# Gated slot attention after the FFN: logits and read-out share one PSUM tensor, and three engines get new orders

## The reference

```python
q = _swish((x @ Wq).reshape(b, t, H, K)); k = _swish((x @ Wk).reshape(b, t, H, K))   # H = 4, K = 64
v = (x @ Wv).reshape(b, t, H, V)
f = jax.nn.log_sigmoid((x @ Wf).reshape(b, t, H, M)) / 8.0
s = 1.0 - jnp.exp(f)
def step(carry, inp):                       # over t, one sequence has 512 steps
    hk = hk * ge[:, :, None, :] + k_t[..., :, None] * s_t[..., None, :]
    logits = jnp.einsum('bhk,bhkm->bhm', q_t * scale, hk)
    p = jax.nn.softmax(logits, axis=-1)
    hv = hv * ge[..., :, None] + s_t[..., :, None] * v_t[..., None, :]
    o_t = jnp.einsum('bhm,bhmv->bhv', p, hv)
o = o * jax.lax.rsqrt(jnp.mean(o * o, axis=-1, keepdims=True) + 1e-5) * g_norm_w
return o.reshape(b, t, H * V) @ Wo
```

## Time and profile before

| | |
|---|---|
| Median of 3 runs | 3388.84 us (3388.57 to 3389.33) |
| The profiled execution: its own time | 3388.84 us |
| its span | 3387.1 us |
| Attention phase, first to last o_raw | 1465.2 to 2408.7 us, 128 operations |
| Busy over the whole span | TensorE 94%, VectorE 78%, ScalarE 49%, GpSimd 38% |
| Granted TensorE clock in 100 us stretches of 1500 to 2400 us | 1.00 |

### The profile page before, as it was taken

One profiled execution on the slowest core, in us unless ns is written; L12 is line 12 of the kernel. 1 busy time (PEld: TensorE's weight loads), 2 busy tenths in 40 slices (PEclk: granted clock), 3 DMA queues, 4 the chain that ended last, 5 costly groups with the idle time before them and its releaser, 6 DMA issues. The chain is left out here.

```text
span 3387.1 us, 102619 instructions
## 1 busy us (share of the span) xinstructions
PE 3176.5 (94%) x36736; PEld 2723.2 (80%) x36736; DVE 2655.2 (78%) x4369; ACT 1669.7 (49%) x4554; POOL 1302.7 (38%) x2170
## 2 busy tenths in 40 slices
PE   5999999999989999889999999999799999999999
PEld 4888888888866666578888888888588888888888
DVE  7999999999962323268888888888699999999998
ACT  3333333333325656578888888888333333333332
POOL 3333333333324343345555555555333333333332
PEclk9999999999989999989999999999799999999999
DMA  3111111111115555533333333333111111111111
GB/s 85 54 54 51 56 51 53 53 53 54 51 52 200 195 200 195 194 93 109 102 107 107 102 106 108 102 107 103 55 53 56 51 53 54 51 56 51 56 51 46
DMA packets 224965, 290.57 MB, mean 86 GB/s; under 512 B 25460, under 2 KB 191732, under 8 KB 224888
## 3 DMA queue, kind: packets, MB, share of 16 engines
q1 hardware_dynamic: 224888, 289.52, 27.0%
HBM read 171.97 MB, written 117.44 MB: 85 GB/s over the span
## 5 line engine op out<-in xcount | busy, mean ns | idle before, releaser
L578 PE MATMUL mid_ps<-xT_hl,w_hl 128*128 128x128 f16 x12288 | 728.7, 219 | 0.0
L425 PE MATMUL res_ps<-w_hl,midT_hl 128*128 128x256 f16 x6144 | 712.5, 273 | 1.2 <-DVE x_out L546 1.2
L578 PEld LDWEIGHTS mid_ps<-xT_hl,w_hl 128*128 128x128 f16 x12288 | 697.9, 98 | 0.5
L382 POOL TENSOR_TENSOR var_eps<-moments,eps_col 128x1 f32<-128x1 f32 x384 | 110.1, 287 | 1481.7 <-DVE moments L378 1481.7
L425 PEld LDWEIGHTS res_ps<-w_hl,midT_hl 128*128 128x128 f16 x6144 | 589.6, 98 | 65.5 <-DVE midT_hl L533 1.7
L486 ACT ACTIVATE midT_hl<-mid_ps 128x1024 f16<-128x1024 f32 x256 | 262.2, 1024 | 695.9 <-PE mid_ps L589 695.9
L512 DVE TENSOR_TENSOR_SCAN runmax<-restart,logits_ps 128x1024 f32<-128x1024 f32 x256 | 581.4, 2271 | 3.5 <-PE logits_ps L567 3.4
L397 ACT ACTIVATE xn_hl<-xc,rstd 128x256 f16<-128x256 f32 x384 | 194.2, 506 | 432.9 <-POOL rstd L387 351.6
L372 DVE BATCH_NORM_STATS2 stats<-x_in 128x6 f32<-128x256 f32 x384 | 161.8, 421 | 294.7 <-DMA x_in<-x 290.0
L533 DVE SCALAR_TENSOR_TENSOR midT_hl<-mid_ps,midT_hl 128x1024 f16<-128x1024 f32 x256 | 313.6, 1225 | 15.6 <-ACT midT_hl L486 7.8
L517 DVE TENSOR_TENSOR step<-runmax 128x1024 bf16<-128x1024 f32 x256 | 315.4, 1232 | 7.9
(11 more groups left out here) (143 smaller groups left out, 6188.9 us busy)
## 6 DMA issues: line engine op xcount, KB each, us to landing
projected<-qkfv_out SPq DMA_DIRECT2D x128, 512.0 KB, 2.9
qkv<-projected SPq DMA_DIRECT2D x128, 384.0 KB, 3.4
x<-x_out SPq DMA_DIRECT2D x256, 128.0 KB, 1.8
x_in<-x SPq DMA_DIRECT2D x256, 128.0 KB, 2.2
x_res<-x SPq DMA_DIRECT2D x256, 128.0 KB, 2.1
x_in<-in_L_attn_x SPq DMA_DIRECT2D x128, 128.0 KB, 2.0
x_res<-in_L_attn_x SPq DMA_DIRECT2D x128, 128.0 KB, 2.1
gate<-projected SPq DMA_DIRECT2D x128, 128.0 KB, 3.1
```

The source lines that it names most:

```text
L425: last = nc.tensor.matmul(dst, left(lp, k), right(rp, k), start=(k == 0 and lp == rp), stop=(k == blocks - 1 and lp == 1))
L578: nc.tensor.matmul(mid_ps[t.slot][:, cols], w1_hl[:, wp, k, cols], xT_hl[:, t.ring, xp, k], start=(c % PER_BANK == 0 and k == 0 and wp == xp),
```

## The change

Logits and read-out share the first 256 columns of one PSUM tensor, bank_rows; `logits` of tile s then waits for o_raw of tile s-2 (which has read them) and `read_out` of tile s-1 for logit of tile s. The transposes of o and the decay column share another, bank_16: `transpose_o` waits for the decay column to be read, the column sums of tile s+2 for oT of tile s-3. Their waits before are gone. The lists of ScalarE, VectorE and TensorE are in another order: ScalarE squares before it copies bank_T; VectorE adds and decays Hk before it masks; TensorE makes the logits before the transposes of k and S, and the state update before A and B. No operation is added or dropped, and GpSimd's and SyncE's lists stay.

```diff
--- before.py
+++ after.py
@@ -725,15 +725,14 @@
             def fb(name, shape, dt=f32):
                 return scope.enter_context(nc.sbuf_tensor(name, shape, dt))
 
-            bank_logits = psum(scope, "bank_logits", BANK)
+            bank_rows = psum(scope, "bank_rows", BANK)
             bank_pair = psum(scope, "bank_pair", 2 * BANK)
             bank_T = psum(scope, "bank_T", BANK)
             bank_state = psum(scope, "bank_state", BANK)
             bank_G = psum(scope, "bank_G", BANK)
-            bank_o = psum(scope, "bank_o", BANK)
+            bank_16 = psum(scope, "bank_16", BANK)
             bank_ends = psum(scope, "bank_ends", BANK)
-            L_ps, col_ps = bank_logits[:, 0:D], bank_logits[:, D:D + PAIRS]
-            o_ps, oT_ps = bank_o[:, 0:D], bank_o[:, D:2 * D].bitcast(f16)
+            oT_ps = bank_16[:, 0:BANK].bitcast(f16)[:, 0:2 * D]
             out_ps, PtT_ps = bank_ends[:, 0:D], bank_ends[:, D:2 * D]
             G_ps, decay_ps = bank_G[:, 0:D], bank_G[:, D:2 * D]
 
@@ -920,7 +919,7 @@
                                                  ).then_inc(S["decay_rows_made"], 1)
                             after_chunk(act, S["decay_col_done"], t, LATER)
                             after_chunk(act, S["Hv_made"], t, LATER, lag=4)
-                            nc.scalar.activation(decay_col[:, t.ring], col_ps, ACT.Exp
+                            nc.scalar.activation(decay_col[:, t.ring], bank_16[:, 0:PAIRS], ACT.Exp
                                                  ).then_inc(S["decay_col_made"], 1)
 
                     def evacuate_T(t):
@@ -963,8 +962,8 @@
                         after(act, S["proj_done"], t, lag=2)
                         nc.scalar.activation(oT[:, t.slot], oT_ps, ACT.Copy).then_inc(S["oT_made"], 1)
 
-                    pipeline(act, [(evacuate_PtT, -1), (evacuate_T, 1), (square, -2), (gate_abs, 4),
-                                   (gate_softplus, 4), (softmax_exp, 0), (o_high, -2), (evacuate_oT, -3),
+                    pipeline(act, [(gate_abs, 4), (evacuate_PtT, -1), (square, -2), (gate_softplus, 4),
+                                   (evacuate_T, 1), (softmax_exp, 0), (o_high, -2), (evacuate_oT, -3),
                                    (gate_high, 4), (exp_sums, 2)],
                              tiles, base, UNROLL, LONGEST_LAG)
 
@@ -1009,7 +1008,7 @@
                         after(dve, S["L_done"], t)
                         after(dve, S["expG_made"], t)
                         after(dve, S["prob_made"], t, lag=2)
-                        nc.vector.scalar_tensor_tensor(logit[:, t.slot], L_ps, QK_SCALE,
+                        nc.vector.scalar_tensor_tensor(logit[:, t.slot], bank_rows[:, 0:D], QK_SCALE,
                                                        expG[:, t.ring], ALU.mult, ALU.mult
                                                        ).then_inc(S["logit_made"], 1)
                         after(dve, S["logit_made"], t)
@@ -1061,7 +1060,7 @@
                         after(dve, S["o_done"], t)
                         after(dve, S["inv_total_made"], t)
                         after(dve, S["o_norm_made"], t, lag=2)
-                        nc.vector.tensor_tensor(heads_of(o_raw[:, t.slot]), heads_of(o_ps),
+                        nc.vector.tensor_tensor(heads_of(o_raw[:, t.slot]), heads_of(bank_rows[:, 0:D]),
                                                 per_head(inv_total[:, t.slot]), ALU.mult
                                                 ).then_inc(S["o_raw_made"], 1)
 
@@ -1085,7 +1084,7 @@
                                                        ).then_inc(S["att_res_added"], 1)
 
                     pipeline(dve, [(divide_o, -2), (decay_Hv, 0), (sum_squares, -2), (scale_logits, 0),
-                                   (gate_logsig, 4), (mask_AB, 1, 2), (add_states, 0), (decay_Hk, 1), (o_low, -2),
+                                   (gate_logsig, 4), (add_states, 0), (decay_Hk, 1), (mask_AB, 1, 2), (o_low, -2),
                                    (invert_totals, 0), (finish, -4), (make_St, 2)],
                              tiles, base, UNROLL, LONGEST_LAG)
 
@@ -1127,16 +1126,16 @@
                         head_products(1, lambda r, a: kT_StT[r, t.ring, 1, a], lambda r, a: PtT[r, t.slot, a],
                                       S["B_done"])
 
-                    def with_state(t, dst, left, which, made, inner, right, done):
+                    def with_state(t, left, which, made, inner, right, done):
 
                         after_chunk(pe, made, t, LATER)
                         for a in range(PAIRS):
                             if t.chunk:
-                                nc.tensor.matmul(dst[:, a * P:(a + 1) * P], left[:, a],
+                                nc.tensor.matmul(bank_rows[:, a * P:(a + 1) * P], left[:, a],
                                                  state[:, t.slot, which, a], start=True, stop=True)
                             for z in range(2):
                                 at = a * P + z * HD
-                                last = nc.tensor.matmul(dst[:, at:at + HD], inner[:, z, a * P:(a + 1) * P],
+                                last = nc.tensor.matmul(bank_rows[:, at:at + HD], inner[:, z, a * P:(a + 1) * P],
                                                         right[:, at:at + HD], start=(t.chunk == 0),
                                                         stop=True,
                                                         skip_group_check=True)
@@ -1145,18 +1144,16 @@
                     def logits(t):
                         after(pe, S["AB_masked"], t)
 
-                        after_last_chunk(pe, S["decay_col_made"], t, LATER, lag=-1)
-                        after(pe, S["logit_made"], t, lag=1)
-                        with_state(t, L_ps, pairs_of(qkv[:, t.ring, 0]), 0, S["Hk_made"], masked[:, t.slot, :, 0],
+                        after(pe, S["o_raw_made"], t, lag=2)
+                        with_state(t, pairs_of(qkv[:, t.ring, 0]), 0, S["Hk_made"], masked[:, t.slot, :, 0],
                                    St[:, t.ring], S["L_done"])
 
                     def read_out(t):
 
                         pe.wait_ge(S["AB_masked"], t.n + 3)
 
-                        after(pe, S["o_raw_made"], t, lag=1)
-                        after(pe, S["oT_made"], t, lag=2)
-                        with_state(t, o_ps, PtT[:, t.slot], 1, S["Hv_made"], masked[:, t.slot, :, 1],
+                        after(pe, S["logit_made"], t, lag=-1)
+                        with_state(t, PtT[:, t.slot], 1, S["Hv_made"], masked[:, t.slot, :, 1],
                                    qkv[:, t.ring, 2], S["o_done"])
 
                     def update_states(t):
@@ -1192,12 +1189,12 @@
                         last.then_inc(S["G_done"], 1)
                         if t.chunk:
 
-                            after(pe, S["logit_made"], t, lag=2)
+                            after(pe, S["oT_made"], t, lag=5)
                             after_last_chunk(pe, S["decay_col_made"], t, LATER, lag=1)
                             for a in range(PAIRS):
                                 for n, (ones, gates) in enumerate(terms):
                                     for part in range(2):
-                                        last = nc.tensor.matmul(col_ps[:, a:a + 1],
+                                        last = nc.tensor.matmul(bank_16[:, a:a + 1],
                                                                 gates[:, part, a * P:(a + 1) * P], ones[:, 0:1],
                                                                 start=(n == 0 and part == 0),
                                                                 stop=(n == 1 and part == 1))
@@ -1207,7 +1204,7 @@
                         after(pe, S["o_low_made"], t)
 
                         after(pe, S["oT_made"], t, lag=1)
-                        after(pe, S["o_raw_made"], t, lag=-1)
+                        after_last_chunk(pe, S["decay_col_made"], t, LATER, lag=-4)
                         for part in range(2):
                             for k in range(KD):
                                 at = (part * KD + k) * P
@@ -1232,8 +1229,8 @@
                                                        ident32[:, :])
                         last.then_inc(S["PtT_done"], 1)
 
-                    pipeline(pe, [(transpose_kSt, 1), (logits, 0), (transpose_o, -3), (products_A, 1),
-                                  (products_B, -1), (update_states, 0), (log_gate_sums, 2), (project_out, -4),
+                    pipeline(pe, [(logits, 0), (transpose_kSt, 1), (transpose_o, -3), (update_states, 0),
+                                  (products_A, 1), (products_B, -1), (log_gate_sums, 2), (project_out, -4),
                                   (read_out, -1), (transpose_Pt, 0)],
                              tiles, base, UNROLL, LONGEST_LAG)
             scope.close()
```

## The result

| | before | changed |
|---|---|---|
| Median, 4 runs each | 3388.7 us (3387.78 to 3389.33) | 3422.59 us (3420.39 to 3427.73) |
| Ratio | 1 | 1.0102, 95% interval 1.0085 to 1.0119 |
| Span of the profiled execution | 3387.1 us | 3421.5 us |
| Four steps c0 to c3 | 29.88 us | 31.13 us |

The change costs 34 us, 1.0%. The forecast was slower, by 75 us. The first rival, the decay of Hk not blocked, had said 3427 us.

What follows compares the result with a forecast made beforehand. It took a ring through S, transposes, copy, square, sum and VectorE's remaining step as the bound. Four steps, 32.24 against 29.88 us, 2.36 more, times 32 is 75.5: 3388.84 + 75 = 3464 us, range 3413 to 3488.

Steps and rivals of the forecast that it cites:

- Four steps c0 to c3: Attention-phase steps, one tile each, named by the chunk whose logits they make: 32.24 us forecast against 29.88, times 32.
- The first rival: Decay of Hk not blocked by Pt, so the mask waits for B: 31.08 us per four steps, 3427 us, chance 0.27.
- Logits can't begin ahead of o_raw: Shared PSUM tensor: TensorE's logits wait for o_raw of tile s-2, first matmul 0.56 us after o_raw's start.
- c0: Step making chunk 0's logits, 0.45 us shorter without a state; decay of Hk blocked, mask at 4.98: 7.94 us.
- c2: Step making chunk 2's logits; decay of Hk blocked by Pt, mask at 5.43, read-out behind it: 8.39 us, before 7.40.
- c1: Step making chunk 1's logits; same mask as c2, read-out of chunk 0 without a state: 7.94 us.
- Here Pt starts 0.08 ahead of it: GpSimd's Pt at 4.51 precedes VectorE's decay of Hk at 4.59, which is blocked and ends at 5.52.
- c3: Step making chunk 3's logits, without update, state_sum or Hk; column sums wait for oT: 7.97 us, before 7.16.
- VectorE's own tail is not later: VectorE's work from mask to next o_raw, 2.22 us, ends at 7.65, at most some 0.1 more in c1.
- The column sums: TensorE's column sums wait for oT of the same step, oT's start + 0.82, so 5.46 at the earliest.
- The other new waits: Read-out on this step's logits, transposes of o on the previous step's decay column: 3 us or more old, cost nothing.
- The recovered stall (faster): Rival: mask and oT are ready before TensorE, only TensorE's own ring is left: 0.46 us less, 3374 us, chance 0.06.

Runs made afterwards that it cites:

- Run 5: The kernel before with the three new orders and old PSUM tensors, plus one wait of logits of tile s for o_raw of tile s-2: 3443.88 us, ratio 1.0169.
- run 2: The kernel before with the three new orders of the change alone, old PSUM tensors and waits: 3344.5 us, ratio 0.9865.
- Run 4: The changed kernel with two one-column reciprocals on VectorE ahead of the decay of Hk, to push it behind Pt's start: 3449.33 us, ratio 1.0182.
- run 6: The kernel before with the three new orders and old PSUM tensors, plus one wait of the column sums for oT: 3337.54 us, ratio 0.9855.
- run 1: The changed kernel with the three old orders, so the shared PSUM tensors and their waits alone: 3402.93 us, ratio 1.0046.
- Run 7: The kernel before with one exchange on ScalarE, the square ahead of the copy of the transposes: 3381.67 us, ratio 0.9986.
- run 3: The changed kernel with VectorE's old order, the mask ahead of state_sum and the decay of Hk: 3544.26 us, ratio 1.0462.
- run 10: The kernel before with VectorE's new order alone, the mask behind state_sum and the decay of Hk: 3486.25 us, ratio 1.0297.
- run 9: The changed kernel with GpSimd made to start Pt after the decay of Hk, gate_low after o_low, own decay after S: 3406.74 us, ratio 1.0055.

## Why the prediction was right or wrong

*Direction: right, and most of the mechanism.* Logits can't begin ahead of o_raw (forecast at 0.56, measured 0.51), the chain update, state_sum, decay, mask has no slack, and the read-out waits for the mask in c0 and c2. Run 5 puts a price on the first link, the one wait on o_raw: 99 us against run 2. The changed kernel, whose logits start 0.17 earlier than those of run 5, is 78 us above run 2.

*Size: wrong, 75 us for 34.* The step that failed is the order in which two operations start in c2 and c1, "Here Pt starts 0.08 ahead of it". Pt was right (4.51 forecast, 4.51 measured). The decay was worked out at 4.59 and came at 4.47; 0.10 of that is the transposes of o, charged with 0.32, their distance to A in the old order, where they take 0.22 ahead of the update. So the decay came 0.04 ahead of Pt (0.05 in c1), took 0.43, and the blocked side was GpSimd. The mask started at 4.94 and not at 5.43. Run 4 shows the case that was priced: with the decay pushed behind Pt the mask starts at 5.45 and c2 takes 8.30 us, against 8.39 forecast. A margin of 0.08 us between two estimates good to 0.1 was no ground for a chance of 0.55 against 0.27.

*What this step is worth.* Four steps were overestimated by 1.11 us (32.24 against 31.13): c2 by 0.58, c3 by 0.22, c1 by 0.20, c0 by 0.11. By run 4 the failed step is 0.61 of it, 20 of the 41 us by which the time was missed. Smaller terms make the other 0.50, 16 us. The last 5 or 6 us come from multiplying by 32: 1.25 us a group give 40 us and 34 were measured, as the first and last groups of the phase are shorter.

*c1: 7.74 for 7.94.* "VectorE's own tail is not later" failed here. With the mask at 4.94, the tail from the mask to o_raw is 2.80 and not 2.22, as S was held by GpSimd for 0.93, and it sets the step.

*c3: 7.75 for 7.97.* The column sums waited for oT as forecast, but start 0.63 after oT's start; the 0.82 was that of another stage's matmul, the read-out. *c0: 7.83 for 7.94*, caught as forecast. From the read-out to o_raw are 1.59 us and not 1.65.

*The first rival* had 31.08 us for four steps against 31.13 measured, with c0 too short by 0.31 (it was caught) and c3 too long by 0.22: its total, and so its 3427 us, is nearer than its parts, which is luck.

*The other new waits*, which "cost nothing": no wait of the changed kernel's trace speaks against it. *The column sums*: priced as on the path in c3; run 6 shows that under the new orders that wait is free, run 1 that under the old ones it costs 16 us.

*The recovered stall (faster) was a rival at 0.06 because of its chain.* Run 7 shows that the wait of the earlier trace rows was worth 5 us by itself. But run 2 shows that the orders were worth 43 us: what they needed was logits that need not wait for the end of o_raw. The forecast did not cost the parts separately, and so missed that the change holds a gain and a larger loss.

The Trainium skill's page "SBUF — State Buffer", section "Who interferes with whom", says that the order of issue decides who is blocked. Both cases shown here agree: the second to start was held, 0.95 against 0.43 for VectorE in c0, 0.97 against 0.73 for GpSimd in c2. It was held for less than the full wait: VectorE's decay ends 0.29 after Pt, not 0.43, and Pt 0.58 after the decay, not 0.73.

## What to carry to other kernels

When a buffer is shared, write out which engine's next step it ties to which, since the same two PSUM tensors cost 16 us under one order and 78 (3344.5 to 3422.6) under another. A long wait is worth what the next wait behind it leaves: here 5 us of 113.7. Where two engines start operations that exclude each other within 0.1 us, price both outcomes as equally likely, or order them with a semaphore.

## What the runs showed of the hardware that was not expected

TensorE's granted clock fell to the lower level for a part of single steps in four kernels: 33 steps of run 3, 13 of run 10 (its last two steps not counted), 10 of run 4 and one at the start of run 9. In the middle of the phase such a step is 1.4 to 3.0 us longer than its like at 1.00. The kernel before and the changed one, with idle gaps of TensorE up to 0.42 and 0.70 us, have no such step between 1500 and 2380 us. The gap ahead of the step does not settle it alone. In run 3 it was 1.36 us ahead of slow and full-speed steps c2 alike; in run 1 a gap of 1.05 us in nearly every c3 never lowered the clock, while in run 4 steps with gaps of up to 0.89 us were followed by it ten times. What does settle it stays open. A change that adds idle time to TensorE can so cost more than that time.

A race of 0.02 us between GpSimd and VectorE fits the two levels of time of run 2, 3336 and 3351 us, from one execution to the next. Only an execution of the slower level has a trace.
